# Reciprocal denominators go to the heads' rows through memory in place of a matmul; keys are spread by 8 transfers per group in place of 16

## The chip, the core and the metric

One Trainium2 chip, one of its NeuronCores. The metric is the device time of one execution of the kernel in microseconds (us). The engines are named as the profile names them: PE (TensorE matmul), PEld (TensorE weight load), DVE (VectorE), ACT (ScalarE), POOL (GpSimd), SP (SyncE, here only an issuer of transfers).

## What is computed

8192 tokens (128 sequences of 64) with 128 features: a layernorm, cross attention with 16 heads of width 8 against a context of the same size, a residual; then a layernorm and a feed-forward layer in which each token goes to the one of 8 experts with the largest router logit, and a residual. Cut to what matters here:

```python
q = split_heads(layernorm(x) @ Wq.T + bq)      # 16 heads, width 8
k = split_heads(ctx @ Wk.T + bk)
v = split_heads(ctx @ Wv.T + bv)
scores = einsum('bhqd,bhkd->bhqk', q, k) / sqrt(8)
out = einsum('bhqk,bhkd->bhqd', softmax(scores), v)
x = x + merge_heads(out) @ Wo.T + bo
n = layernorm(x);  e = argmax(n @ Wr.T + br)
x = x + (relu(n @ W1[e].T + b1[e]) @ W2[e].T + b2[e])
```

All data are float32.

## The kernel before

**Stage 1** (about 0 to 68 us) runs over 16 groups of 512 tokens (`GW`; four tiles of 128, `GT`). It normalises x, turns it, and makes Q, K and V for the group with four kinds of matmul (L886, L890, L899, L907); ACT copies them to `QT`, `KT` and `V`.

**Stage 2** (about 68 to 352 us) is a pipeline written out by hand. In step n of 81, tile n of 128 tokens (two sequences) gets its scores (PE, L877), their maximum and the difference to it (DVE, L698 and L706) and the exponential (ACT, L546). In the same step PE turns the exponentials of tile n-2 in two halves of four transposes (L918); ACT copies each half out of the one PSUM bank that both use (L529, L538), so the second half waits for the copy of the first. Then PE makes numerators (L994) and denominators (L1003) of tile n-3.

Denominators of a group of four tiles g are collected in one PSUM bank: row 8h+t holds those of head h, tile t. DVE takes the reciprocal of the whole bank (`RD`, L702, 128x128) once per group, in step 4g+7 (`L_RD`), between its maximum and its subtraction. One step later the first of the group's four tiles needs them: for each tile, PE multiplies a constant selector `C_SEL` by `RD` (L948), which copies row 8h+t to all eight rows of head h, into PSUM bank 7; DVE multiplies that by the numerators `NUM` (L722, `OT`). One step later again PE applies Wo (L952) and DVE adds the residual (L725). Tile m is multiplied in step m+8 (`L_MUL`) and added in step m+9 (`L_X1`). Behind that follow, with eight tiles per batch, the second layernorm's sums, the router's logits (transposes L977, copy L535 to `X1T`, matmul L959), ranks (L966, L968) and the rows' places, and POOL scatters the rows to a DRAM scratch `rows` (L466). DVE works in program order; so do PE, ACT and POOL.

**Keys.** The scores' moving operand `KM` is block diagonal per head: SP copies, for each group s, each head's eight partitions of `KT` to their slot, 16 transfers of 8 partitions x 2 KB (L341), in a loop over s. Group s may be copied once the scores of group s-2 are done. Group 0's 16 copies are issued by POOL (L410). `KM` has room for two groups, and is filled with zeros by POOL in stage 1.

**SP's queue** after stage 1: the copies of keys for s = 1 to 15; then the pad rows and the experts' first weights `WE` (L348), `W2` (L350), seven pads to `rows` (L353), and the blocks of sorted rows, one transfer per block of 128 rows with a register load before each (L362).

**Stage 3** (from step 67, `F0`, about 335 us, to the end) handles 71 blocks of 128 sorted rows. Up to step 80 its blocks are interleaved with what is left of stage 2, one block per step: DVE normalises (L832), PE turns (L1009) and multiplies (L1024, L1037), ACT copies the expert's weights (L559) and applies relu (L563), and POOL scatters the result to `out` (L473).

Of the kernel before, what the change touches and what calls it, by code (L numbers as in the profile page):

```python
# [44 lines left out]
C_ID, C_TRI, C_ONE, C_OWN, C_DEN, C_SEL, C_PREF, C_BASE, C_LIM, C_BLK, C_EPS, C_1H, C_LE, C_END = np.cumsum(  # L45
    [0, P, P, P, 2 * DK, GT * 64, GT * P, E, E, NT, NB, 1, ST, E * E]).tolist()
# [5 lines left out]
def constants():  # L52
# [12 lines left out]
    for t in range(GT):  # L65
        c[:, C_SEL + P * t:C_SEL + P * (t + 1)] = (p[:, None] // DK == p[None, :] // DK) & (p[:, None] % DK == t)
# [100 lines left out]
def build(nc, x, ctxT, wts, we, w2, con, pad, ids, out):  # L167
# [3 lines left out]
    rows = nc.dram_tensor("rows", (ROWS, RW), f32).ap()  # L171

    ctx = ExitStack()
    with ctx:
# [20 lines left out]
        BQK = W[:, W_BQ:W_BQ + 2]  # L195
        WR, BR = W[:, W_R:W_R + E], W[:, W_BR:W_BR + E]

        X1T = sb("X1T", P, 4, 2, P)
# [37 lines left out]
        RD = sb("RD", P, 2, P)  # L236
        OT = sb("OT", P, 2, P)
# [37 lines left out]
        con_in, w_in, ids_in, w2_in = sem("con_in"), sem("w_in"), sem("ids_in"), sem("w2_in")  # L275
# [15 lines left out]
        num_kept, rdx_done, wr_mm, wr_ready = (sem(n) for n in ("num_kept", "rdx_done", "wr_mm", "wr_ready"))  # L291
# [19 lines left out]
        def _(sp):  # L311

            def load_group(s):
                def go(before):
# [17 lines left out]
            def spread(s):  # L332
                sp.wait_ge(q_kept, s.n + 1)
                sp.sem_inc(spread_go, 1)
                need(sp, s_done, GT * (s.n - 1))
                sp.sem_inc(spread_go, 1)
                at = bass.ds(s.n * GW, GW)
                for g in range(2):
                    for j in range(HP):
                        own = slice(SEQ * g + DK * j, SEQ * g + DK * (j + 1))  # L340
                        sp.dma_start(KM[own, s.r, j, :], KT[own, at]).then_inc(km_in[s.r], 16)  # L341
            steps(sp, 1, NG, 2, spread, peel=2)

# [25 lines left out]
            for n in range(NB1 - E):  # L369
                load_block(0)(Step(n // RR, n % RR, RR))  # L370
# [16 lines left out]
        def _(pool):  # L387
# [8 lines left out]
            def stage1(n):  # L396
# [90 lines left out]
        def _(act):  # L487
# [4 lines left out]

            def root(n, dst, src, slots, mv, sd, rstd):
# [4 lines left out]
            def keep(t):  # L498
# [11 lines left out]
                if isinstance(s.n, int) and s.n == 0:  # L510
                    act.wait_ge(w_in, 16)
# [9 lines left out]
            def softmax(s):  # L521
# [8 lines left out]
                for i in range(4):  # L530
                    j = s.batch(M_TR + 2 * i)
                    if j is not None:
                        act.wait_ge(xt2_done, 4 * j + i + 1)
                        need(act, lgp_done, 4 * j - 3 + i)
                        nc.scalar.copy(X1T[:, i].rearrange("p t d -> p (t d)"), bank(6)[:, 2 * P:4 * P]).then_inc(x1t_ready, 1)  # L535
# [45 lines left out]
        def _(dve):  # L581
# [110 lines left out]
            def stage2(s):  # L692
# [17 lines left out]
                need(dve, rdx_done, min(n - L_MUL + 1, NT))  # L710
# [154 lines left out]
        def _(pe):  # L865
# [3 lines left out]
            nc.tensor.matmul(bank(7)[:, D:D + E], C[:, C_ONE:C_ONE + P], WR, start=True, stop=True).then_inc(wr_mm, 1)  # L869

# [12 lines left out]
            def stage1(s):  # L883
                pe.wait_ge(ct_in[s.r], 16 * (s.it + 1))
                need(pe, k_kept, s.n - 1)
                nc.tensor.matmul(bank(4 + s.r % 2), WK, CT[:, s.r, :], start=True, stop=True).then_inc(k_done, 1)  # L886
# [16 lines left out]
                if isinstance(s.n, int) and s.n == NG - 1:  # L903
                    pe.wait_ge(km_first, 16 * H)
                    scores(0)
                need(pe, q_kept, s.n - 1)
                nc.tensor.matmul(bank(2 + s.r % 2), WQ, XNT[:, s.r % 2, :], start=True, stop=True).then_inc(q_done, 1)  # L907
# [13 lines left out]
            def stage2(s):  # L921
                n = s.n
                if 1 <= n < NT:
                    grp, t = divmod(n, GT)
                    if t == 0 and grp:
                        pe.wait_ge(km_in[grp % 2], 16 * H * ((grp + 1) // 2))
# [10 lines left out]
                need(pe, ot_ready, min(n - L_MUL, NT))  # L937
# [159 lines left out]
```

## Time and profile before

| | |
|---|---|
| median of 3 runs | 499.24 us (497.53 to 502.27) |
| the profiled execution | 501.58 us, of which the profile's span is 499.8 us |
| PE busy | 461.1 us (92% of the span) |
| DVE busy | 408.2 us (82%) |
| ACT busy | 313.0 us (63%) |
| POOL busy | 240.6 us (48%) |
| DMA | 33.98 MB, mean 68 GB/s |
| granted TensorE clock | mean 0.98; a slice near 80 us at 0.5 |

Busy times are of one execution on the chip. A busy PE is not PE at its peak: ends of matmuls are modelled, so the timeline of single instructions and what each waited for say more than the share. Times of rows count from the start of the span.

A row of the timeline has start and duration in us, engine, line, operation, output and input, and in brackets how long its engine sat idle before it and what released it. A row of the windows has, for one stretch, its length, the busy us and instructions of PE, PEld, DVE, ACT and POOL in this order, the granted clock, the DMA engines' busy share and GB/s. A row of one line has the duration of an issue (min, median, max in ns), or the us from the start of an issue to its landing. A row of the page's DMA issues ends with the KB of one and the same us. A row of waits has who waited for whom: us in total, times, longest.

### The profile page before, as it was taken

How to read it: one execution, taken by the hardware profiler on the slowest of the kernel's cores; microseconds unless marked ns; L12 is line 12 of the kernel's file. 1: busy time of each engine (PE TensorE's matmuls, PEld its weight loads, DVE VectorE, ACT ScalarE, POOL GpSimd, SP SyncE). 2: the span in 40 equal slices, each digit the busy share in tenths (PEclk: the TensorE clock that was granted, in tenths of full speed). 3: DMA queues.
4: the chain of work that ended last, by engine and by line, in shares of the span. 5: the costliest groups of instructions: out<-in, count | busy, mean ns of one | idle time of the engine just before them, and what ended most of it. 6: DMA issues, size and time to landing. Idle time of an engine off the chain costs nothing. (4 is left out here: it accounts for less than half of the span.)

```text
span 499.8 us, 18728 instructions
## 1 busy us (share of the span) xinstructions
PE 461.1 (92%) x6467; PEld 347.9 (70%) x6467; DVE 408.2 (82%) x1061; ACT 313.0 (63%) x589; POOL 240.6 (48%) x390
## 2 busy tenths in 40 slices
PE   3999978899999999999999999988789999999990
PEld 1666634456666666666666666668779999999990
DVE  4999864677899899998999999958878887887870
ACT  1677764666666666666666665665557777777760
POOL 1548620222232464555645645554767645455551
PEclk9999995999999999999999999999999999999996
DMA  8356300011000111111111115722223332222100
GB/s 281 108 148 177 90 11 12 14 22 20 18 17 18 33 41 30 38 38 36 35 34 33 39 41 201 264 71 76 77 66 103 101 87 66 72 61 74 39 32 0
DMA packets 32752, 33.98 MB, mean 68 GB/s; under 512 B 6675, under 2 KB 26006, under 8 KB 32416
## 3 DMA queue, kind: packets, MB, share of 16 engines
q1 hardware_dynamic: 27840, 24.10, 18.7%
q0 software_dynamic: 4832, 8.80, 5.3%
q8 instruction: 53, 0.87, 0.8%
q14 instruction: 27, 0.22, 0.2%
HBM read 19.14 MB, written 9.99 MB: 58 GB/s over the span
## 5 line engine op out<-in xcount | busy, mean ns | idle before, releaser
L451 POOL TENSOR_TENSOR VP<-BIG,C 128x128 f32<-128x128 f32 x128 | 56.1, 458 | 136.5 <-PE PS L1003 132.7
L918 PEld LDWEIGHTS PS<-C,SB 128*128 128x128 f32 x512 | 54.6, 142 | 68.2 <-ACT SB L546 32.5
L698 DVE TENSOR_REDUCE MX<-PS 128x16 f32<-128x1024 f32 x64 | 78.3, 1223 | 29.1 <-PE PS L877 27.7
L473 POOL DMA_INDIRECT out<-SB,BIG x71 | 70.1, 987 | 52.6 <-DVE SB L849 44.7
L918 PE MATMUL PS<-C,SB 128*128 128x128 f32 x512 | 85.1, 290 | 7.5 <-ACT PT L529 7.2
L546 ACT ACTIVATE SB<-SB 128x1024 f32<-128x1024 f32 x64 | 67.7, 1057 | 23.7 <-DVE SB L706 22.0
L706 DVE TENSOR_TENSOR SB<-PS,MX 128x1024 f32<-128x1024 f32 x64 | 77.4, 1210 | 1.7
L1024 PE MATMUL PS<-BIG,KM 128*128 128x128 f32 x568 | 76.8, 277 | 0.3 <-issue 0.2
L1037 PE MATMUL PS<-KM,SB 128*128 x568 | 75.8, 277 | 0.6 <-ACT SB L563 0.6
L466 POOL DMA_INDIRECT rows<-X,DESTI x64 | 64.2, 1003 | 19.6 <-issue 14.1
L877 PE MATMUL PS<-KM,BIG 64*64 64x512 f32 x512 | 71.2, 629 | 0.8 <-ACT BIG L517 0.8
L559 ACT COPY KM<-BIG 128x644 f32 x71 | 51.7, 729 | 30.2 <-PE PS L1024 24.8
L1024 PEld LDWEIGHTS PS<-BIG,KM 128*128 128x128 f32 x568 | 69.7, 192 | 1.4 <-issue 1.2
L1037 PEld LDWEIGHTS PS<-KM,SB 128*128 128x128 f32 x568 | 69.1, 192 | 1.2 <-issue 0.8
L538 ACT COPY PT<-PS 128x512 f32<-128x512 f32 x64 | 37.5, 586 | 36.7 <-PE PS L918 36.6
L529 ACT COPY PT<-PS 128x512 f32<-128x512 f32 x64 | 37.4, 585 | 36.2 <-PE PS L918 32.8
L838 DVE TENSOR_TENSOR SB<-PS,KM 128x512 f32<-128x512 f32 x71 | 49.0, 690 | 5.4 <-PE PS L1024 2.4
L563 ACT ACTIVATE SB<-SB 128x512 f32<-128x512 f32 x71 | 44.6, 628 | 10.0 <-DVE SB L838 9.7
L994 PE MATMUL PS<-PT,VP 128*32 128x64 f32 x2048 | 42.3, 223 | 0.2
L1003 PE MATMUL PS<-PT,C 128*32 128x128 f32 x1024 | 40.3, 276 | 1.1 <-DVE RD L702 0.7
L994 PEld LDWEIGHTS PS<-PT,VP 128*32 128x32 f32 x2048 | 31.9, 110 | 11.1 <-issue 11.0
L846 DVE TENSOR_TENSOR SB<-PS,KM 128x128 f32<-128x128 f32 x71 | 20.6, 291 | 18.1 <-PE PS L1037 17.2
(122 smaller groups left out, 699.0 us busy)
## 6 DMA issues: line engine op xcount, KB each, us to landing
BIG<-rows SPq DMA_DIRECT2D x71, 66.0 KB, 1.9
X<-in_x SPq DMA_DIRECT2D x16, 256.0 KB, 3.3
PT<-in_ctxT SPq DMA_DIRECT2D x16, 256.0 KB, 3.0
KM<-BIG SPq DMA_DIRECT2D x240, 16.0 KB
BIG<-in_we SPq DMA_DIRECT2D x1, 2576.0 KB, 11.5
KM<-in_w SPq DMA_DIRECT2D x1, 2048.0 KB, 15.9
out<-SB,BIG POOLq DMA_INDIRECT x71, 2.3
rows<-X,DESTI POOLq DMA_INDIRECT x64, 2.4
```

The costliest lines, as they stand in the source:

```text
L451: last = nc.gpsimd.tensor_tensor(dst, v, own, ALU.mult)
L466: nc.gpsimd.indirect_dma_start(out=rows, out_offset=bass.IndirectOffsetOnAxis(ap=DESTI[:, j % 2, t:t + 1], axis=0), in_=X[:, j * ST + t, : ...
L473: nc.gpsimd.indirect_dma_start(out=out, out_offset=bass.IndirectOffsetOnAxis(ap=RT[:, s.r, ID:ID + 1].bitcast(i32), axis=0), in_=YO[:, s.r ...
L546: nc.scalar.activation(SB[:, n % 3, :], SB[:, n % 3, :], ACT.Exp, scale=SCALE).then_inc(exp_done, 1)
L559: nc.scalar.copy(WS[:, s.r % 4, :], WE[:, bass.ds(ex, 1), :].rearrange("p e f -> p (e f)")).then_inc(ws_ready, 1)
L698: nc.vector.tensor_reduce(MX[:, n % 2, :], sc, axis=AX.X, op=ALU.max).then_inc(mx_done, 1)
L706: nc.vector.tensor_tensor(SB[:, n % 3].rearrange("p (h k) -> p h k", h=H), sc, MX[:, n % 2, :].unsqueeze(2).to_broadcast([P, H, SEQ]), ALU ...
L877: last = nc.tensor.matmul(bank(2 * (n % 2) + g)[SEQ * b:SEQ * (b + 1), :], QT[rows_g, n * P + SEQ * b:n * P + SEQ * (b + 1)], KM[rows_g, g ...
L918: last = nc.tensor.transpose(bank(4)[:, i * P:(i + 1) * P], SB[:, n % 3, hp * P:(hp + 1) * P], ident)
L994: nc.tensor.matmul(bank(6)[32 * c:32 * c + 32, at:at + SEQ], VP[:, m % 2, b, 2 * c + z, :], PT[:, m % 2, 2 * c + z, SEQ * b:SEQ * b + SEQ] ...
L1024: last = nc.tensor.matmul(bank(2 + b.r % 2)[:, c * P:(c + 1) * P], WS[:, b.r % 4, c * P:(c + 1) * P], XT[:, b.r % 2, :], start=True, stop= ...
L1037: last = nc.tensor.matmul(bank(4 + b.r % 2)[:, 0:D], HT[:, b.r % 2, c * P:(c + 1) * P], w, start=c == 0, stop=c == FC - 1)
```

## The change

The selector matmul (L948) goes away, and its constant `C_SEL` with it (512 columns, 256 KB of the constants' transfer). In its place SP does, once per group, `ratios(g)`: it waits for the reciprocal, writes `RD` (64 KB) to a DRAM scratch `ratio`, waits for that to land, and reads it back with each of a head's four rows repeated to the head's eight partitions, into `RDX` (128 partitions x 2 KB, 256 KB). DVE waits for that second transfer before it multiplies, and reads `RDX` in place of PSUM. `RDX` has room for two groups. `ratios(s-2)` stands behind the keys' copies of group s; `ratios(14)` stands before the pads, and `ratios(15)` behind the first eight loads of blocks.

The columns of Wq and Wk are put in another order on chip (two copies by ACT at the start, into `RDX`, which is free then), with which one partition of each head lies every 8 partitions. So a transfer `KM[j:P:8]` <- `KT[j:P:8]` takes two heads at once with 16 partitions, and there are 8 per group. The biases come in the same order by two transfers of their own. SP's loop over groups is written out. `WE` and `W2` are issued by ACT in place of SP, in steps 58 and 61. `X1T` has two slots in place of four, and PE waits for `W2` two steps later.

```diff
-C_ID, C_TRI, C_ONE, C_OWN, C_DEN, C_SEL, C_PREF, ...
+C_ID, C_TRI, C_ONE, C_OWN, C_DEN, C_PREF, ...
...
+    ratio = nc.dram_tensor("ratio", (2, P, P), f32).ap()
...
-        BQK = W[:, W_BQ:W_BQ + 2]
+        BQK = sb("BQK", P, 2)
+        def turned(w):
+            return w.rearrange("p (g j d) -> p g d j", g=2, j=HP)
...
-        X1T = sb("X1T", P, 4, 2, P)
+        X1T = sb("X1T", P, 2, 2, P)
...
+        RDX = sb("RDX", P, 2, GT, P)
...
+                        for g in range(2):
+                            own = slice(SEQ * g, SEQ * (g + 1))
+                            sp.dma_start(BQK[own, :], wts[own, W_BQ:W_BQ + 2].rearrange("(j d) b -> d j b", j=HP)).then_inc(b_in, 16)
                         sp.dma_start(IDS[:], ids).then_inc(ids_in, 16)
...
-            def spread(s):
-                sp.wait_ge(q_kept, s.n + 1)
+            def ratios(g):
+                sp.wait_ge(rd_done, g + 1)
+                need(sp, rdx_in[g % 2], 16 * (g // 2))
+                sp.dma_start(ratio[g % 2], RD[:, g % 2, :]).then_inc(rd_out[g % 2], 16)
+                need(sp, ot_ready, GT * (g - 1))
+                sp.wait_ge(rd_out[g % 2], 16 * (g // 2 + 1))
+                of = ratio[g % 2].rearrange("(h a) q -> h a q", a=DK)[:, 0:GT, :].rearrange("h t q -> h (t q)")
+                sp.dma_start(RDX[:, g % 2].rearrange("p t q -> p (t q)"), of.unsqueeze(1).to_broadcast([H, DK, GT * P])).then_inc(rdx_in[g % 2], 16)
+
+            for s in range(1, NG):
+                sp.wait_ge(q_kept, s + 1)
                 sp.sem_inc(spread_go, 1)
-                need(sp, s_done, GT * (s.n - 1))
+                need(sp, s_done, GT * (s - 1))
                 sp.sem_inc(spread_go, 1)
-                at = bass.ds(s.n * GW, GW)
-                for g in range(2):
-                    for j in range(HP):
-                        own = slice(SEQ * g + DK * j, SEQ * g + DK * (j + 1))
-                        sp.dma_start(KM[own, s.r, j, :], KT[own, at]).then_inc(km_in[s.r], 16)
-            steps(sp, 1, NG, 2, spread, peel=2)
+                for j in range(HP):
+                    sp.dma_start(KM[j:P:HP, s % 2, j, :], KT[j:P:HP, s * GW:(s + 1) * GW]).then_inc(km_in[s % 2], 16)
+                if s >= 2:
+                    ratios(s - 2)
...
             sp.dma_start(PADR[:], pad).then_inc(padr_in, 16)
-            sp.dma_start(WE[:], we).then_inc(we_in, 16)
-            sp.wait_ge(s_done, NT - GT)
-            sp.dma_start(W2, w2).then_inc(w2_in, 16)
+            ratios(NG - 2)
             sp.wait_ge(padr_in, 16)
...
             for n in range(NB1 - E):
+                if n == 8:
+                    ratios(NG - 1)
                 load_block(0)(Step(n // RR, n % RR, RR))
...
-                    for k in range(4 * (n - 8), 4 * (n - 7)):
-                        g, j = divmod(k, HP)
-                        own = slice(SEQ * g + DK * j, SEQ * g + DK * (j + 1))
-                        pool.dma_start(KM[own, 0, j, :], KT[own, 0:GW]).then_inc(km_first, 16)
+                    for j in range(2 * (n - 8), 2 * (n - 7)):
+                        pool.dma_start(KM[j:P:HP, 0, j, :], KT[j:P:HP, 0:GW]).then_inc(km_first, 16)
...
+            act.wait_ge(w_in, 16)
+            for k, w in enumerate((WQ, WK)):
+                last = nc.scalar.copy(RDX[:, 0, k, :].rearrange("p (g d j) -> p g d j", g=2, d=DK), turned(w))
+            last.then_inc(w_turned, 1)
...
                 softmax(Step(n // ST, n % ST, ST))
+                if n == NT - 6:
+                    for r in range(2):
+                        act.wait_ge(km_in[r], 16 * HP * (NG // 2 - 1 + r))
+                    act.dma_start(WE[:], we).then_inc(we_in, 16)
+                if n == NT - 3:
+                    act.wait_ge(s_done, NT - GT)
+                    act.dma_start(W2, w2).then_inc(w2_in, 16)
...
                     dve.wait_ge(od_done, GT * g + GT)
+                    need(dve, rdx_in[g % 2], 16 * (g // 2))
                     nc.vector.reciprocal(RD[:, g % 2, :], bank(5)[:, P * (g % 2):P * (g % 2) + P]).then_inc(rd_done, 1)
...
-                need(dve, rdx_done, min(n - L_MUL + 1, NT))
...
                 if 0 <= m < NT:
+                    g, t = divmod(m, GT)
                     dve.wait_ge(num_kept, m + 1)
-                    nc.vector.tensor_tensor(OT[:, m % 2, :], bank(7)[:, 0:P], NUM[:, m % 8, :], ALU.mult).then_inc(ot_ready, 1)
+                    dve.wait_ge(rdx_in[g % 2], 16 * (g // 2 + 1))
+                    nc.vector.tensor_tensor(OT[:, m % 2, :], RDX[:, g % 2, t, :], NUM[:, m % 8, :], ALU.mult).then_inc(ot_ready, 1)
...
+            pe.wait_ge(w_turned, 1)
...
-                m = n - L_MUL
-                if 0 <= m < NT:
-                    g, t = divmod(m, GT)
-                    pe.wait_ge(rd_done, g + 1)
-                    nc.tensor.matmul(bank(7)[:, 0:P], C[:, C_SEL + P * t:C_SEL + P * (t + 1)], RD[:, g % 2, :],
-                                     start=True, stop=True).then_inc(rdx_done, 1)
...
-            pe.wait_ge(w2_in, 16)
             pe.wait_ge(tab_ready, 1)
             for n in range(F0, STEPS):
                 k = n - F0
+                if k == 2:
+                    pe.wait_ge(w2_in, 16)
```

## Rows read from the trace of the kernel before

**Rows 1.** windows of busy time by engine, eight steps of stage 2
```profile
178.80:210.90 32.10, 31.97 (x579) 21.45 (x578) 30.12 (x64) 20.40 (x37) 17.62 (x38) 1.00 0.16 36
```

**Rows 2.** timeline of two steps: PE, PEld and ACT
```profile
200.32 1.09 PE L877 MATMUL PS<-KM,BIG 64*64 64x512 f32 x8
...
201.34 0.66 PE L918 MATMUL PS<-C,SB 128*128 128x128 f32 x4
...
201.84 0.39 PE L948 MATMUL PS<-RD,C 128*128 128x128 f32 x2
...
202.04 0.58 ACT L529 COPY PT<-PS 128x512 f32<-128x512 f32 x1 [0.79 <-PE PS L918]
...
202.67 0.42 PEld L918 LDWEIGHTS PS<-C,SB 128*128 128x128 f32 x4 [0.24 <-ACT PT L529]
...
206.00 0.58 ACT L529 COPY PT<-PS 128x512 f32<-128x512 f32 x1 [0.79 <-issue]
...
206.63 0.42 PEld L918 LDWEIGHTS PS<-C,SB 128*128 128x128 f32 x4
```

**Rows 3.** timeline, ACT and PEld in a step with the ranks' matmuls
```profile
222.13 0.58 ACT L529 COPY PT<-PS 128x512 f32<-128x512 f32 x1 [0.73 <-PE PS L918]
...
222.95 0.42 PEld L918 LDWEIGHTS PS<-C,SB 128*128 128x128 f32 x4
```

**Rows 4.** timeline of DVE around two reciprocals
```profile
194.71 0.95 DVE L702 RECIPROCAL RD<-PS 128x128 f32<-128x128 f32 x1
...
197.52 1.22 DVE L698 TENSOR_REDUCE MX<-PS 128x16 f32<-128x1024 f32 x1 [0.20 <-PE PS L877]
...
199.92 0.28 DVE L722 TENSOR_TENSOR OT<-PS,NUM 128x128 f32<-128x128 f32 x1
...
201.48 1.22 DVE L698 TENSOR_REDUCE MX<-PS 128x16 f32<-128x1024 f32 x1 [0.88 <-PE PS L877]
...
210.92 0.95 DVE L702 RECIPROCAL RD<-PS 128x128 f32<-128x128 f32 x1
...
216.05 0.28 DVE L722 TENSOR_TENSOR OT<-PS,NUM 128x128 f32<-128x128 f32 x1
```

**Rows 5.** the page's DMA issues: the experts' first weights
```profile
BIG<-in_we SPq DMA_DIRECT2D x1, 2576.0 KB, 11.5
```

**Rows 6.** line L325, context loads, 256 KB each
```profile
DMA to landing us min/median/max: 2.6/3.0/6.2
```

**Rows 7.** waits of SP's queue, 374 to 400 us: last pad's write
```profile
SPq L382 <- DMA rows<-BIG: 1.1, 1, 1.1
```

**Rows 8.** line L466, 300 to 325 us: scatters while WE, W2 load
```profile
DMA to landing us min/median/max: 2.3/6.0/7.5
```

**Rows 9.** lines L341, and L362 from 326 to 336 us: SP's issues
```profile
L341 SPq DMA_DIRECT2D KM<-BIG x240: 645/646/1555, 54.5 to 301.9; - x120
...
L362 SPq DMA_DIRECT2D BIG<-rows x8: 350/352/365, 326.8 to 335.0; - x8
```

**Rows 10.** timeline, 304 to 341 us: SP, ACT, DVE around last reciprocals
```profile
304.40 1.57 SPq L348 DMA_DIRECT2D BIG<-in_we  x1
...
305.28 1.06 ACT L546 ACTIVATE SB<-SB 128x1024 f32<-128x1024 f32 x1 [0.92 <-DVE SB L706]
...
307.71 0.95 DVE L702 RECIPROCAL RD<-PS 128x128 f32<-128x128 f32 x1
...
313.55 0.28 DVE L722 TENSOR_TENSOR OT<-PS,NUM 128x128 f32<-128x128 f32 x1
...
325.18 0.95 DVE L702 RECIPROCAL RD<-PS 128x128 f32<-128x128 f32 x1
...
329.27 0.29 DVE L722 TENSOR_TENSOR OT<-PS,NUM 128x128 f32<-128x128 f32 x1 [1.47 <-PE PS L959]
...
337.00 0.95 DVE L702 RECIPROCAL RD<-PS 128x128 f32<-128x128 f32 x1
...
340.07 0.29 DVE L722 TENSOR_TENSOR OT<-PS,NUM 128x128 f32<-128x128 f32 x1 [0.68 <-PE PS L968]
```

More of the change, by code:

```diff
@@ L42 @@
 SCALE = float(1.0 / np.sqrt(np.float32(DK)))
-C_ID, C_TRI, C_ONE, C_OWN, C_DEN, C_SEL, C_PREF, C_BASE, C_LIM, C_BLK, C_EPS, C_1H, C_LE, C_END = np.cumsum(
-    [0, P, P, P, 2 * DK, GT * 64, GT * P, E, E, NT, NB, 1, ST, E * E]).tolist()
+C_ID, C_TRI, C_ONE, C_OWN, C_DEN, C_PREF, C_BASE, C_LIM, C_BLK, C_EPS, C_1H, C_LE, C_END = np.cumsum(
+    [0, P, P, P, 2 * DK, GT * 64, E, E, NT, NB, 1, ST, E * E]).tolist()
 (W_Q, W_K, W_V, W_BQ, W_BK, W_O, W_BV, W_BO, W_R, W_BR, W_END) = np.cumsum(
@@ L64, in constants @@
                 c[half, C_DEN + 64 * t + 32 * z + 16 * z + DK * r + t:C_DEN + 64 * t + 32 * z + 16 * z + DK * (r + 1):GT] = 1
-    for t in range(GT):
-        c[:, C_SEL + P * t:C_SEL + P * (t + 1)] = (p[:, None] // DK == p[None, :] // DK) & (p[:, None] % DK == t)
     c[:, C_PREF:C_PREF + E] = E - np.arange(E)
@@ L272, in bank @@
             return PS[:, 512 * k:512 * (k + n)]
-        con_in, w_in, ids_in, w2_in = sem("con_in"), sem("w_in"), sem("ids_in"), sem("w2_in")
+        con_in, w_in, w_turned, b_in, ids_in, w2_in = sem("con_in"), sem("w_in"), sem("w_turned"), sem("b_in"), sem("ids_in"), sem("w2_in")
         x_in, ct_in = sems("x_in", 4), sems("ct_in", 4)
@@ L290, in build @@
         stat2, mv2, inv_step, scaled = (sem(n) for n in ("stat2", "mv2", "inv_step", "scaled"))
-        num_kept, rdx_done, wr_mm, wr_ready = (sem(n) for n in ("num_kept", "rdx_done", "wr_mm", "wr_ready"))
+        num_kept, wr_mm, wr_ready = (sem(n) for n in ("num_kept", "wr_mm", "wr_ready"))
+        rd_out, rdx_in = sems("rd_out", 2), sems("rdx_in", 2)
         seed_step, sd2_done, inv2_done = sem("seed_step"), sem("sd2_done"), sem("inv2_done")
@@ L330, in _ @@
             sp.wait_ge(zeroed, 8)
-            def spread(s):
-                sp.wait_ge(q_kept, s.n + 1)
+            def ratios(g):
[8 more added lines that the diff above has]
+                sp.wait_ge(q_kept, s + 1)
                 sp.sem_inc(spread_go, 1)
-                need(sp, s_done, GT * (s.n - 1))
+                need(sp, s_done, GT * (s - 1))
                 sp.sem_inc(spread_go, 1)
-                at = bass.ds(s.n * GW, GW)
-                for g in range(2):
-                    for j in range(HP):
-                        own = slice(SEQ * g + DK * j, SEQ * g + DK * (j + 1))
-                        sp.dma_start(KM[own, s.r, j, :], KT[own, at]).then_inc(km_in[s.r], 16)
-            steps(sp, 1, NG, 2, spread, peel=2)
+                for j in range(HP):
+                    sp.dma_start(KM[j:P:HP, s % 2, j, :], KT[j:P:HP, s * GW:(s + 1) * GW]).then_inc(km_in[s % 2], 16)
+                if s >= 2:
+                    ratios(s - 2)
             for r in range(2):
-                sp.wait_ge(km_in[r], 16 * H * (NG // 2 - 1 + r))
+                sp.wait_ge(km_in[r], 16 * HP * (NG // 2 - 1 + r))
             sp.dma_start(PADR[:], pad).then_inc(padr_in, 16)
-            sp.dma_start(WE[:], we).then_inc(we_in, 16)
-            sp.wait_ge(s_done, NT - GT)
-            sp.dma_start(W2, w2).then_inc(w2_in, 16)
+            ratios(NG - 2)
             sp.wait_ge(padr_in, 16)
@@ L510, in keep @@
                 if isinstance(s.n, int) and s.n == 0:
-                    act.wait_ge(w_in, 16)
+                    act.wait_ge(b_in, 16 * 2)
                 act.wait_ge(k_done, s.n + 1)
@@ L533, in softmax @@
                         act.wait_ge(xt2_done, 4 * j + i + 1)
-                        need(act, lgp_done, 4 * j - 3 + i)
-                        nc.scalar.copy(X1T[:, i].rearrange("p t d -> p (t d)"), bank(6)[:, 2 * P:4 * P]).then_inc(x1t_ready, 1)
+                        need(act, lgp_done, 4 * j - 1 + i)
+                        nc.scalar.copy(X1T[:, i % 2].rearrange("p t d -> p (t d)"), bank(6)[:, 2 * P:4 * P]).then_inc(x1t_ready, 1)
                 if 2 <= n < NT + 2:
@@ L885, in stage1 @@
                 need(pe, k_kept, s.n - 1)
-                nc.tensor.matmul(bank(4 + s.r % 2), WK, CT[:, s.r, :], start=True, stop=True).then_inc(k_done, 1)
+                nc.tensor.matmul(bank(4 + s.r % 2), RDX[:, 0, 1, :], CT[:, s.r, :], start=True, stop=True).then_inc(k_done, 1)
                 pe.wait_ge(xn_done, s.n + 1)
@@ L903, in stage1 @@
                 if isinstance(s.n, int) and s.n == NG - 1:
-                    pe.wait_ge(km_first, 16 * H)
+                    pe.wait_ge(km_first, 16 * HP)
                     scores(0)
                 need(pe, q_kept, s.n - 1)
-                nc.tensor.matmul(bank(2 + s.r % 2), WQ, XNT[:, s.r % 2, :], start=True, stop=True).then_inc(q_done, 1)
+                nc.tensor.matmul(bank(2 + s.r % 2), RDX[:, 0, 0, :], XNT[:, s.r % 2, :], start=True, stop=True).then_inc(q_done, 1)
             steps(pe, 0, NG, 4, stage1, peel=4, tail=4)
@@ L925, in stage2 @@
                     if t == 0 and grp:
-                        pe.wait_ge(km_in[grp % 2], 16 * H * ((grp + 1) // 2))
+                        pe.wait_ge(km_in[grp % 2], 16 * HP * ((grp + 1) // 2))
                     need(pe, sub_done, n - 1)
@@ L936, in stage2 @@
                 need(pe, x1_done, min(n - L_X1, NT))
-                need(pe, ot_ready, min(n - L_MUL, NT))
+                if 0 <= n - L_X1 < NT:
+                    pe.wait_ge(ot_ready, n - L_X1 + 1)
                 j = s.routing(M_TOP)
@@ L958, in stage2 @@
                             at = 2 * P + (ST * (j % 2) + 2 * i + t) * E
-                            last = nc.tensor.matmul(bank(7)[:, at:at + E], X1T[:, i, t, :], WR, start=True, stop=True)
+                            last = nc.tensor.matmul(bank(7)[:, at:at + E], X1T[:, i % 2, t, :], WR, start=True, stop=True)
                         last.then_inc(lgp_done, 1)
```

## The prediction

> **What bounds the kernel now.** I read the windows first. In the middle of stage 2, eight steps take 32.1 us, 4.0 us a step, and PE is busy for 31.97 of them at full clock while DVE is busy for 30.12 [rows 1]. Both are near their limit, so a busy share doesn't say what an edit is worth; the timeline does. The reader is to see in [rows 2] that the matmul to be removed stands in a hole. PE ends the first half of the transposes at 201.34 + 0.66 = 202.00. ACT copies it from 202.04 to 202.62, and only then, at 202.67, can the second half begin, after 0.24 us of idle that ends with that copy. From half to half 1.33 us pass, and the selector matmul, Wo and the transposes of X lie inside. In the next step, where two logit matmuls lie in the hole, the copy ends at 206.58 and the second half starts at 206.63: copy and PE's work end together. Only where the ranks' matmuls are added does PE outlast the copy: the copy ends at 222.71, the second half starts at 222.95 [rows 3]. That is one step in eight.
>
> Then DVE. The reciprocal ends at 195.66 and the first product of its group starts at 199.92, 4.26 us later; the next pair is 211.87 and 216.05, 4.18 us [rows 4]. DVE's idle in eight steps is the 0.20 before 197.52 and the 0.88 before 201.48, 1.08 us in all (the other steps show none). These gaps are what two transfers in a row have to fit into.
>
> **The change, part by part.** The sum is made on the profiled execution, 501.6 us; it lies 2.3 us above the median of the runs, 499.2.
>
> *The selector matmul, 64 times.* Its two passes are busy for 0.39 us [rows 2], and it starts 0.16 us before the transposes end, so part of that overlaps with its neighbours; I take half, 0.2 us, as what it adds to PE's work. With it gone, seven steps of eight wait for ACT's copy exactly as before: 0. In the rank step it gives back at most 222.95 - 222.71 = 0.24, of which 0.05 is the copy's handover [rows 3]: 0.19 us, for about seven batches 1.3 us. DVE's product reads the core's memory in place of PSUM; no row shows this to be shorter, and I take 0.28 us for both [rows 4].
>
> *The two transfers, in the middle.* The write of 64 KB: the last pad, 66 KB from SP to DRAM, was waited for 1.1 us after its issue [rows 7], and an issue takes 0.35 [rows 9]: 1.45 us. From above, a scatter of 66 KB, POOL's own work in it, takes 2.3 us in quiet [rows 8]. The read of 256 KB in pieces of 2 KB: the context's loads have size and pieces, 2.6 to 3.0 us [rows 6]. Handovers DVE to SP, SP to SP and back: 0.04 to 0.05 each in [rows 2]; I take 0.3 for the three. So 4.35 us from below (1.45 + 2.6 + 0.3) and 5.6 from above (2.3 + 3.0 + 0.3); I take 4.8, near the rows of the same issuer. What may it be? In eight steps DVE meets the wait twice, and with its idle gone the gaps are 4.26 - 0.20 and 4.18, 8.24 us. PE's eight steps are 32.1 - 0.19, and DVE without idle needs 32.1 - 1.08, so 0.89 us of delay is free: 2 x trip = 9.13, a trip of 4.57 is hidden. With 4.8 the loss is 0.46 us in eight steps, with 5.6 it is 2.1, with 4.35 nothing and the 0.19 remain. For seven times eight steps: 3 us, between -1.3 and 14. I take 4, since other transfers use the same engines in some of the trips. SP has nothing else to do then; what is queued behind its wait is the next group's keys. What waits behind DVE's wait is Wo of the step after and the next maximum.
>
> The Trainium skill (DMA: Bandwidth & Descriptors, Anatomy of one DMA) puts a transfer at about 2.0 us and its bytes by 436 GB/s. An estimate by it is 2.15 + 2.6 + 0.3 = 5.05 us, and a loss of 7 us in place of 4; the section also says that completion is slowest where the target is the chip's DRAM, which would put the write above the pad's 1.45 us.
>
> *The keys.* An issue takes 0.645 us on SP [rows 9]. Sixteen were at least 10.3 us per group, eight are 5.2, or 10.3 if twice the rows cost twice. Group g+3 may start when the scores of step 4g+7 are done, but now SP first serves the reciprocal of that step: up to 1.7 us to its start (the maximum takes 1.2 [rows 4]), 0.95, 1.6 for the write, 0.4 to issue the read, 4.7 us in all. With the issues and up to 3 us to land that is 13 us (18 at twice the cost); five steps less one set of scores, 5 x 4.0 - 1.1 = 19 us, are there. Hidden: 0. Without that cover PE would stand at the group's first scores.
>
> *The start.* The constants shrink by 256 KB; at the rate of the 2576 KB that landed in 11.5 us [rows 5] that is 1.1 us of transfer, if the start is bound by it. Two small transfers and two weight copies on ACT come in. I take -0.5, between -1 and +1.
>
> *WE moved to ACT, with reciprocal 13.* ACT issues it behind the exponential of step 58, which ends at 306.34 [rows 10]. The issue took SP 1.57 us and now holds ACT's copies of step 59 for that long. More dearly, the load then meets the write of reciprocal 13 (ends at 308.66). In the kernel before, scatters of the same size that met these loads took 6.0 us in the middle and up to 7.5, against 2.3 [rows 8]. So the write takes about 6.5, lands at 315.3, and the read 3 to 4 more: the trip is some 10 to 11 us. The product that waits stands at 313.55, 4.9 us after the reciprocal: 5.5 us late. ACT's 1.57 lies beside that, and about 0.5 is absorbed: +5. From below +1 (the transfers don't hinder each other), from above +8.
>
> *Reciprocal 14.* It ends at 326.13; its product starts at 329.27 after an idle of 1.47 [rows 10]. A trip of 5 to 7 us (W2, issued by ACT in step 61, is then still loading) ends 2 to 4 us after that, and DVE's idle in that step and what a step without scores leaves free take most: +1.5, between 0 and 3.
>
> *Reciprocal 15.* Here SP itself is late. Pads and loads now stand behind ratios(14). The write lands and the read is issued 2 us after 326.13; seven pads at the 0.35 to 0.6 of an issue, 4 us: the first block's load goes out at about 332, which the first block just bears (it is wanted in step 67, the step of reciprocal 15). Eight loads come at (335.0 - 326.8) / 7 = 1.17 us [rows 9], to 341.5. But the reciprocal ends at 337.95 and its product stood at 340.07 [rows 10]. Write at 341.5, landed with the read at 346: 6 us late, 3 if SP were free. DVE's blocks stand behind the product, and PE and ACT wait for them; nothing there covers 6 us. +5.5, between 2.5 and 7.
>
> *The last steps of stage 2.* After the last scores a step is a loop between PE and DVE through bank 7 (the product at 329.27 was released by PE). A matmul less is 0.2 us in about eight steps: -1.5, at least 0.
>
> Sum, with the rank steps' 1.3 us inside the 4: -0.5 + 4 + 5 + 1.5 + 5.5 - 1.5 = +14 us, 515.6 on the profiled execution and 513.2 on the median; the prediction is for the median, rounded up to 514.
>
> **Rivals.**
>
> *PE gives the matmul back (faster).* If the copy did not end the hole, every step would be 0.2 us shorter: 64 x 0.2 = 13 us, 487. For it: PE is busy for 31.97 of 32.1 us [rows 1]. Against it: the 0.24 us of idle on the copy [rows 2], half of all steps; and DVE has only 1.08 us in eight steps to follow. It decides if the trip stays below 4.57 us and PE's hole isn't bound by the copy. 0.1, some gain in other places included.
>
> *Hidden (within 1%).* The trips are 4.3 us, and in the tail the loads hinder them little: -1.3 - 0.5 + 1 + 0 + 2.5 - 1.5 = 0: 499 to 503. For it: the pad's 1.45 us and the 2.6 us at the low end [rows 6, 7]. 0.2.
>
> *Much slower.* The trip is 5.6 in the middle (14 us), and the loads hold reciprocal 13 to the end of WE: 14 - 0.5 + 8 + 3 + 7 = 31 us, 530. The Trainium skill (DMA: Bandwidth & Descriptors, Queues, rings and completion order) has each DMA engine change between queues only after a whole packet of some 9 to 17 descriptors, by which the write would stand behind all of WE's rows. By rows, WE lands 11.5 us after its issue [rows 5] near 306.4, so at about 318, and the read ends at 321: 7.5 us late in place of 5.5. 0.15, with it a loss of PE's clock in the new idle.
>
> **Numbers.** The forecast has 0.55, and 503 to 526 as its own range; faster 0.1, hidden 0.2, much slower 0.15. The range is to leave out no more than 0.2: faster and a part of the much slower, 498 to 527. About 1%, 5 us, is what can be told from no change: faster 0.12, within 0.18, slower 0.7.
>
> **What would show it.** In the profile after: DVE's product of each group's first tile idle before it, released by a DMA into `RDX`, 0.3 to 1 us, and the idle before the next maximum gone; eight steps of 32.5 us; PE with idle between the halves of the transposes; SP's keys never waited for by L877; one wait of 5 us at step 60 while WE loads and one of 5 to 6 at step 68. If the waits on `RDX` are absent in the middle, the trip was overestimated; if eight steps take under 31.5 us, the hole was read wrongly; if step 60 shows no long wait, the two queues don't hinder each other.

## The result, and the profile after

| | before | changed |
|---|---|---|
| median | 499.21 us (497.53 to 502.52, 6 runs) | 518.67 us (517.06 to 526.37, 6 runs) |
| ratio | | 1.0399, 95% interval 1.0354 to 1.0444 |
| profiled execution, span | 501.58, 499.8 us | 518.43, 516.6 us |

The change makes the kernel 4.0% slower, 19.5 us in the medians. Forecast were 514 us, 498 to 527. All ratios compare fast executions with fast ones of the kernel before, measured beside them, so they differ a little from the quotient of the medians; the 526.37 us is a slow one.

First the middle, the same eight steps as in all that follows (from the maximum of tile 24 to that of tile 32); columns as in [rows 1].

```profile
162.80:196.00 33.20, 31.23 (x562) 20.13 (x563) 30.32 (x64) 20.17 (x37) 17.79 (x38) 1.00 0.18 55
```

33.2 us where [rows 1] has 32.1. PE has 0.74 us less of work in them and takes 1.1 us longer. Not every eight steps are alike: from the maximum of tile 40 to that of tile 48 they take 32.2 us and the next eight 33.9. Over the 48 steps from 8 to 56 it is 33.0 us for eight, and 32.1 in the kernel before. The hole between the transposes' halves is as in [rows 2]: first half to 212.97, copy to 213.58, second half from 213.63, in the changed kernel's timeline:

```profile
212.31 0.66 PE L946 MATMUL PS<-C,SB 128*128 128x128 f32 x4
...
213.00 0.58 ACT L547 COPY PT<-PS 128x512 f32<-128x512 f32 x1
...
213.63 0.42 PEld L946 LDWEIGHTS PS<-C,SB 128*128 128x128 f32 x4 [0.20 <-ACT PT L547]
```

The new wait, in the same view: the reciprocal of step 47, then the first product of its group, then the next maximum, which no longer waits (compare [rows 4]).

```profile
258.79 0.95 DVE L728 RECIPROCAL RD<-PS 128x128 f32<-128x128 f32 x1
...
265.82 0.29 DVE L749 TENSOR_TENSOR OT<-RDX,NUM 128x128 f32<-128x128 f32 x1 [1.82 <-DMA RDX<-ratio]
...
266.43 1.21 DVE L723 TENSOR_REDUCE MX<-PS 128x16 f32<-128x1024 f32 x1
```

From the reciprocal's end to the product are 6.08 us here; over the twelve trips of the middle it is 4.9 to 6.2, 5.5 in the mean, and DVE waits 1.25 us of each. The list of waits has the sum: all 16 groups are waited for.

```profile
DVE OT L749 <- DMA RDX<-ratio: 30.2, 16, 5.7
```

Then the end of stage 2. WE's issue, reciprocal 13, SP's two issues and the product in step 60:

```profile
307.67 0.40 ACTq L589 DMA_DIRECT2D BIG<-in_we  x1
...
310.23 0.95 DVE L728 RECIPROCAL RD<-PS 128x128 f32<-128x128 f32 x1
311.20 0.33 SPq L343 DMA_DIRECT2D ratio<-RD  x1
...
318.02 0.55 SPq L347 DMA_DIRECT2D RDX<-ratio  x1
...
321.60 0.29 DVE L749 TENSOR_TENSOR OT<-RDX,NUM 128x128 f32<-128x128 f32 x1 [5.26 <-DMA RDX<-ratio]
```

SP's next issue comes 6.8 us after that of the write, and PE stands idle for 5.5 us before Wo (L975), which needs the product (timeline of PE):

```profile
322.97 0.77 PE L975 MATMUL PS<-W,OT 128*128 128x128 f32 x2 [5.53 <-DVE PREF L680]
```

Reciprocal 15 in step 67 and its product in step 68:

```profile
348.14 0.95 DVE L728 RECIPROCAL RD<-PS 128x128 f32<-128x128 f32 x1
...
351.21 0.37 SPq L343 DMA_DIRECT2D ratio<-RD  x1
352.93 0.55 SPq L347 DMA_DIRECT2D RDX<-ratio  x1
356.23 0.29 DVE L749 TENSOR_TENSOR OT<-RDX,NUM 128x128 f32<-128x128 f32 x1 [5.71 <-DMA RDX<-ratio]
```

SP issues the write 2.1 us after the reciprocal's end (349.09), since it is still at the eight loads.

Where the time went in the two profiled executions, by how much later the same instruction starts than before (maxima and products of DVE, DVE's first instruction of the last block):

| stretch | later by | of it here |
|---|---|---|
| to the first maximum | +0.1 | +0.1 |
| steps 0 to 4 | -3.9 | -4.0 |
| steps 4 to 59 | +2.5 | +6.4 |
| step 60 (reciprocal 13) | +8.05 | +5.5 |
| steps 61 to 63 | +9.1 | +1.1 |
| steps 64 and 65 (reciprocal 14) | +10.1 | +1.0 |
| steps 66 and 67 | +11.1 | +1.0 |
| step 68 (reciprocal 15) | +16.2 | +5.0 |
| to the last block | +17.1 | +0.9 |

The second line is not the change's doing as far as can be told; without it the lines add up to 21 us. From 75 to 87 us the kernel before ran at a mean clock of 0.57 in its profiled execution (first row) and the changed one at full clock (second row), with the same instructions behind the transposes of 76 us:

```profile
75.00:87.00 12.00, 9.59 (x81) 4.69 (x82) 5.48 (x5) 5.53 (x9) 0.86 (x2) 0.57 0.06 12
```

```profile
75.00:87.00 12.00, 8.83 (x144) 4.79 (x144) 7.98 (x7) 8.00 (x13) 1.74 (x4) 1.00 0.08 23
```

The same window has 0.72 in the profiles of e5 and e10 and 1.00 in that of e2, so kernels with and without the transfers show either. The kernel before comes in both kinds by its mean clock: of its 19 executions measured beside e1, those with a mean clock of 0.991 or 0.992 took 497.6 to 499.2 us, those with 0.981 or 0.982 took 501.4 to 502.7, and the profiled one (501.58 us, 0.982) is of the second kind. On the other side the changed kernel has two stretches at the lower level (1.2 GHz) that the kernel before has not, one around PE's idle in step 60 and one around the wait in step 68 (e1 and e2 below, which have no such wait, show one too, between 333 and 348 us):

```profile
320.00:327.00 7.00, 4.03 (x60) 3.32 (x64) 5.12 (x16) 1.93 (x4) 0.00 (x0) 0.51 0.13 37
347.00:361.00 14.00, 8.16 (x43) 7.52 (x44) 6.74 (x29) 4.16 (x9) 1.27 (x3) 0.52 0.30 78
```

### The profile page after: what moved, and what is told of

It reads as the page before. It is cut to its first block and busy times, and to the rows that moved or that the text cites. A ratio compares the mean times of both kernels' runs of the same rounds, so it can differ in the third digit from the quotient of the medians.

```text
span 516.6 us, 18138 instructions
## 1 busy us (share of the span) xinstructions
PE 454.2 (88%) x6339; PEld 338.9 (66%) x6339; DVE 408.7 (79%) x1061; ACT 312.4 (60%) x591; POOL 237.4 (46%) x382
## 5 line engine op out<-in xcount | busy, mean ns | idle before, releaser
L464 POOL TENSOR_TENSOR VP<-BIG,C 128x128 f32<-128x128 f32 x128 | 57.6, 469 | 143.1 <-PE PS L1026 139.2
L946 PE MATMUL PS<-C,SB 128*128 128x128 f32 x512 | 83.9, 287 | 13.7 <-ACT PT L547 11.1
L1047 PE MATMUL PS<-BIG,KM 128*128 128x128 f32 x568 | 78.8, 281 | 0.3 <-issue 0.2
L479 POOL DMA_INDIRECT rows<-X,DESTI x64 | 64.4, 1006 | 19.5 <-issue 13.1
L1047 PEld LDWEIGHTS PS<-BIG,KM 128*128 128x128 f32 x568 | 71.6, 196 | 1.4 <-issue 1.2
L905 PE MATMUL PS<-KM,BIG 64*64 64x512 f32 x512 | 69.5, 615 | 0.8 <-ACT BIG L535 0.8
L749 DVE TENSOR_TENSOR OT<-RDX,NUM 128x128 f32<-128x128 f32 x64 | 24.0, 375 | 32.1 <-DMA RDX<-ratio 30.2
L975 PE MATMUL PS<-W,OT 128*128 128x128 f32 x128 | 27.9, 301 | 16.7 <-DVE PREF L680 8.6
```

The source lines that it names most:

```text
L464: last = nc.gpsimd.tensor_tensor(dst, v, own, ALU.mult)
L479: nc.gpsimd.indirect_dma_start(out=rows, out_offset=bass.IndirectOffsetOnAxis(ap=DESTI[:, j % 2, t:t + 1], axis=0), in_=X[:, j * ST + t, : ...
L905: last = nc.tensor.matmul(bank(2 * (n % 2) + g)[SEQ * b:SEQ * (b + 1), :], QT[rows_g, n * P + SEQ * b:n * P + SEQ * (b + 1)], KM[rows_g, g ...
L946: last = nc.tensor.transpose(bank(4)[:, i * P:(i + 1) * P], SB[:, n % 3, hp * P:(hp + 1) * P], ident)
L1047: last = nc.tensor.matmul(bank(2 + b.r % 2)[:, c * P:(c + 1) * P], WS[:, b.r % 4, c * P:(c + 1) * P], XT[:, b.r % 2, :], start=True, stop= ...
```

## The experiments

**Is the matmul worth anything?** e1: the kernel before, the matmul out, nothing in its place.

```diff
-                    nc.tensor.matmul(bank(7)[:, 0:P], C[:, C_SEL + P * t:...], RD[:, g % 2, :], ...)
...
-                    nc.vector.tensor_tensor(OT[:, m % 2, :], bank(7)[:, 0:P], NUM[:, m % 8, :], ALU.mult)
+                    nc.vector.tensor_tensor(OT[:, m % 2, :], C[:, C_SEL:C_SEL + P], NUM[:, m % 8, :], ALU.mult)
```

> The kernel before with the selector matmul taken out and nothing in its place: DVE multiplies the numerators by a constant, so the attention's rows are not divided by their denominators (the part left out). Theory (the matmul stood in the hole of ACT's copy): only the rank steps and the last steps get shorter, -1.3 and -1.5 us, so 496 to 499 us, and eight steps of the middle take 31.9 to 32.1 us. Rival (PE sets every step): 64 x 0.2 = 13 us less, about 486 us, and eight steps of 30.5 us.

Measured 501.2 us beside 500.5 for the kernel before, ratio 1.0016 (0.9976 to 1.0056). Windows of the eight steps:

```profile
162.85:194.81 31.96, 30.62 (x562) 19.82 (x562) 30.30 (x64) 20.16 (x37) 17.89 (x38) 1.00 0.15 36
```

PE's busy time falls from 31.97 us [rows 1] to 30.62, 1.35 us, and the stretch only from 32.14 us (the same eight steps, 165.38 to 197.52 before) to 31.96. The rival is gone: a PE busy for 99.6% of the time had 1.35 us of its work in a hole. The rank step's 0.19 us is there. The 1.5 us of the last steps are not seen: from step 59 to 66 the kernel without the matmul gains under 0.1 us on the kernel before, and behind that it has a stretch at the lower level (336 to 345 us) which the kernel before has not.

**Is it the transfers?** e2: the changed kernel with the matmul back; the transposed weights in a tile of their own.

```diff
-                if s >= 2:
-                    ratios(s - 2)
...
-                    nc.vector.tensor_tensor(OT[:, m % 2, :], RDX[:, g % 2, t, :], NUM[:, m % 8, :], ALU.mult)
+                    nc.vector.tensor_tensor(OT[:, m % 2, :], bank(7)[:, 0:P], NUM[:, m % 8, :], ALU.mult)
...
+                    nc.tensor.matmul(bank(7)[:, 0:P], C[:, C_SEL + P * t:...], RD[:, g % 2, :], ...)
```

> The changed kernel with the selector matmul back in place of the two transfers; keys by 8 transfers, turned weights and the weights' loads on ACT stay. Theory (the transfers through memory cost it all): eight steps of 32.1 us, no wait of 5 us in steps 60 and 68, 498 to 502 us in all. Rival (keys' transfers, the turned weights or ACT's issues cost a part): 503 us or more.

498.0 us, ratio 0.9966 (0.9934 to 0.9999), eight steps of 32.1 us. The transfers cost all of it; keys by 8 transfers and the weights' loads on ACT cost nothing that can be seen. Its lead of a third of a percent is at the edge of the interval, too small to be called a gain.

**Is it the trip's length?** e3 leaves out one leg, e4 adds one.

```diff
-                sp.dma_start(ratio[g % 2], RD[:, g % 2, :]).then_inc(rd_out[g % 2], 16)
-                sp.wait_ge(rd_out[g % 2], 16 * (g // 2 + 1))
-                of = ratio[g % 2].rearrange(...)
+                of = ctxT[0:H, 0:GT * P]
```

> The changed kernel without the write to memory and the wait for it: the read follows the reciprocal at once and takes another tensor of the same shape and pieces, so the denominators do not reach the rows (the part left out). The trip becomes about 3.5 us in place of 5.3. Theory (length of the trip against a gap of 4.6 us): no wait on RDX in the middle, eight steps of 31.9 us, 5 to 6 us less there; in step 60 and 68 the waits go down by the write's time, 5 and 2 us; about 505 us in all. Rival (contention of the transfers with others, or the new wait's order costs it, whatever its length): 515 us or more.

```diff
                 sp.dma_start(ratio[g % 2], RD[:, g % 2, :]).then_inc(rd_out[g % 2], 16)
+                sp.wait_ge(rd_out[g % 2], 16 * (2 * (g // 2) + 1))
+                sp.dma_start(ratio[g % 2], RD[:, g % 2, :]).then_inc(rd_out[g % 2], 16)
...
-                sp.wait_ge(rd_out[g % 2], 16 * (g // 2 + 1))
+                sp.wait_ge(rd_out[g % 2], 16 * (2 * (g // 2) + 2))
```

> The changed kernel with the write done twice, one after the other has landed: 1.9 us more per trip. Theory (DVE pays every us beyond what its idle covers, twice in eight steps): eight steps are 3.8 us longer than in the changed kernel, 36 to 37 us; 16 x 1.9 = 30 us more in all, about 548 us, some 5 more where the weights load. Rival (the wait is mostly absorbed by other slack): under 530 us.

e3: 505.9 us, 1.0101 (1.0037 to 1.0164), 31.98 us in eight steps and no wait on `RDX` before step 60. e4: 554.4 us, 1.1053 (1.0983 to 1.1122); its trips are 6.5 to 8.7 us, and eight steps take 38.3 us, or 36.8 in a stretch at full clock. First e3, then two windows of e4:

```profile
162.20:194.18 31.98, 30.63 (x562) 19.83 (x562) 30.32 (x64) 20.18 (x37) 17.90 (x38) 1.00 0.17 53
```

```profile
174.30:212.60 38.30, 32.31 (x562) 21.31 (x563) 29.96 (x65) 20.48 (x37) 18.14 (x38) 0.96 0.17 51
290.40:327.20 36.80, 31.32 (x563) 20.16 (x563) 29.95 (x66) 20.21 (x37) 18.03 (x38) 1.00 0.17 52
```

One leg, two legs, three legs: 31.9, 33.0 and 37.4 us for eight steps in the mean of steps 8 to 56. The first leg is free. The second is paid in part: DVE waits 1.25 us for each trip, and eight steps, with two trips, are 0.9 us longer than before. The third is paid in full: the trips are 2.1 us longer in the mean, and eight steps 4.4 us, of which a lower clock in places has a part. In e3 the read of 256 KB per group still runs, and in e9 below both transfers do, at 32.0 us: it is the wait that costs, not the traffic.

**Is it WE in step 60?** e5 moves the issues of WE and W2 later, e11 puts them back on SP, where they stand behind reciprocal 13.

```diff
-                if n == NT - 6:
+                if n == NT - 4:
...
                     act.dma_start(WE[:], we).then_inc(we_in, 16)
-                if n == NT - 3:
+                if n == NT:
```

> The changed kernel with the issue of WE two steps later (step 60) and that of W2 three steps later (step 64), so that the write of reciprocal 13 has gone before WE starts and WE has landed before that of reciprocal 14. Theory (the 5.3 us wait in step 60 is the write queued beside WE): the trip of reciprocal 13 goes from 10.4 us to about 5.5, the wait in step 60 to under 1 us; W2 now loads beside nothing or beside reciprocal 14's read; 513 to 515 us in all. Rival (something else in step 60 is late, ACT's issue above all): the wait stays, 518 us.

```diff
             sp.dma_start(PADR[:], pad).then_inc(padr_in, 16)
+            sp.dma_start(WE[:], we).then_inc(we_in, 16)
+            sp.wait_ge(s_done, NT - GT)
+            sp.dma_start(W2, w2).then_inc(w2_in, 16)
             ratios(NG - 2)
...
-                    act.dma_start(WE[:], we).then_inc(we_in, 16)
...
-                    act.dma_start(W2, w2).then_inc(w2_in, 16)
```

> The changed kernel with the issues of WE and W2 back on SP, behind the pad's load and ahead of ratios(14), so behind reciprocal 13's transfers; all else as changed. Theory (the 5.3 us wait in step 60 is the meeting of the write with WE, and the loads are done before the blocks' loads start): the trip of reciprocal 13 goes from 10.4 to 5.5 us and nothing takes its place in step 67, where e5 waited 5.9 us; 513 to 514 us in all. Rival (the loads then hinder reciprocal 14 by as much): 517 us or more.

e5: 519.3 us, 1.036 (1.0287 to 1.0433). The cause is confirmed and the gain is not. The trip of reciprocal 13 goes from 10.4 to 5.5 us and the wait to 0.32; but then the first block's rows are waited for. Their load is issued at 343.3 us, while W2 (issued at 337.87, 10.6 us to landing) is still in flight (timeline of DVE in e5):

```profile
321.45 0.38 DVE L749 TENSOR_TENSOR OT<-RDX,NUM 128x128 f32<-128x128 f32 x1 [0.32 <-DMA RDX<-ratio]
...
350.96 0.35 DVE L859 TENSOR_SCALAR BIG<-BIG 128x128 f32<-128x128 f32 x1 [5.92 <-DMA BIG<-rows]
```

By these times the collision moved from step 60 to step 67, where I had not looked. e11: 516.6 us, 1.033 (1.0296 to 1.0363): no wait in step 60 (trip 5.1 us), 1.25 us for the first block, and reciprocal 14 as in the changed kernel. Of the 5.3 us some 2 come back in the median, 3.5 by the ratios, whose intervals overlap.

**Is it SP's order in step 68?** e6 serves reciprocal 15 behind six loads.

```diff
-                if n == 8:
+                if n == 6:
                     ratios(NG - 1)
```

> The changed kernel with reciprocal 15 served behind six loads of blocks in place of eight. Theory (of the 7.1 us of that trip 2.1 are SP's lateness): the trip goes to about 5.1 us, the wait in step 68 from 5.7 to 3.7, 516 to 517 us in all. Rival (SP's order does not matter there, or the later loads of blocks 6 and 7 are then waited for): 518.5 us or more.

519.7 us, 1.0398 (1.0326 to 1.047), and not the expected 516 to 517. The trip goes from 7.1 to 5.2 us and the wait from 5.7 to 3.8, as expected; the time shows nothing that its interval can tell. In the profile the product of step 68 is 14.0 us later than before where it was 16.2, but two steps on it is 16.0 where it was 17.0, so half of the gain is gone by then. SP's lateness was 2 of the 5.7 us, the rest is the trip itself.

**Are the keys late?** e8 spreads them by 16 transfers again.

```diff
-                for j in range(HP):
-                    sp.dma_start(KM[j:P:HP, s % 2, j, :], KT[j:P:HP, ...])
+                for g in range(2):
+                    for j in range(HP):
+                        at = slice(SEQ * g + j, SEQ * (g + 1), HP)
+                        sp.dma_start(KM[at, s % 2, j, :], KT[at, ...])
```

> The changed kernel with the keys spread by 16 transfers of 8 partitions per group as before, everything else as changed. Theory (SP has time for both): PE never waits for keys, the middle's eight steps stay at 33 us, 518 to 520 us; at the end ACT's wait for the last keys ahead of WE may be met, up to 1.5 us. Rival (halving the transfers was what made room for the new ones): keys late for each group, 2 to 3 us per group, 550 us.

520.7 us, 1.0399 (1.0347 to 1.0451), not to be told from the changed kernel. PE never waits for keys in either. The eight steps from tile 24 took 34.2 us and not 33, but from step 4 to 59 it is 228.0 us beside 227.2, so little of that is the keys'. The halving was not needed for SP to serve the new transfers.

**Can the trip be covered?** e7 puts product and residual one step later, e9 the routing too, e10 serves reciprocal 15 behind four loads, e12 adds e11's order.

```diff
-L_MUL = 8
-L_X1 = 9
+L_MUL = 9
+L_X1 = 10
...
-SOON = 2
+SOON = 1
```

(`SOON` is by how many steps the routing of the last two batches runs ahead of the others' place.)

> The changed kernel with product and residual one step later (steps m+9 and m+10, and the last batches' routing one step later with them), so that the trip has a gap of about 8.5 us. Theory (trip against gap): no wait on RDX in the middle, eight steps of 31.97 us, 5 to 6 us less there; in step 60 (now 61) the wait goes from 5.3 to about 2 us, in step 68 (now 69) from 5.7 to about 3; the additional step at the end costs 2 to 3 us; 507 to 511 us in all. Rival (the transfers hurt also where DVE does not wait for them): 514 us or more.

512.9 us, 1.026 (1.0211 to 1.0309). No product of the middle waits any more, and still the eight steps take 33.1 us. My expectation of 32.0 failed. The timeline of DVE in e7 shows another cause: moments (L612 to L620) and seed (L772 to L778) now fall into one step, and the maximum after them, the reciprocal and the subtraction start late; the idle stands in other steps.

```profile
205.19 0.36 DVE L612 TENSOR_TENSOR MS<-STAT 128x8 f32<-128x8 f32 x1
...
207.35 0.17 DVE L778 TENSOR_SCALAR HALF<-VAR 128x8 f32<-128x8 f32 x1
207.55 1.22 DVE L723 TENSOR_REDUCE MX<-PS 128x16 f32<-128x1024 f32 x1
208.69 0.95 DVE L728 RECIPROCAL RD<-PS 128x128 f32<-128x128 f32 x1
...
212.76 1.22 DVE L723 TENSOR_REDUCE MX<-PS 128x16 f32<-128x1024 f32 x1 [1.44 <-PE PS L905]
```

e9 tells that from the transfers: product and residual as in e7, SOON back to 2, all of the routing's offsets one more, so that only the last batches keep e7's places.

```diff
-M_SEED = 18
-M_INV = (19, 20)
+M_SEED = 19
+M_INV = (20, 21)
...
-M_TOP = 21
-M_HOT = 22
-M_RANK = 22
-M_POS = 23
-M_OUT = 23
+M_TOP = 22
+M_HOT = 23
+M_RANK = 23
+M_POS = 24
+M_OUT = 24
```

> The changed kernel with product and residual one step later as in e7_step_later, and also all of the routing's work (square root's seed, top, ranks, places) one step later, so that the moments and the seed are again in different steps. Theory (in e7 eight steps took 33.1 us without any wait on RDX because moments and seed, 2.3 us of DVE, fell into one step right before the reciprocal's 0.95): eight steps go back to about 32.0 us, 507 to 509 us in all. Rival (the transfers themselves slow the other engines down): eight steps stay at 33 us, 512 to 513 us.

505.9 us, 1.012 (1.0093 to 1.0146), and the eight steps:

```profile
162.10:194.10 32.00, 30.73 (x563) 19.89 (x562) 30.44 (x65) 20.21 (x37) 17.52 (x37) 1.00 0.18 55
```

The same DVE work (30.44 us against 30.52 in e7) placed otherwise is worth 1.1 us in eight steps, and 7 us in all. From step 4 to 59 e9 takes 219.8 us, e7 227.9 and the kernel before 220.8: with the trips covered the middle is 1.1 us shorter than before, near the 1.3 us that the rank steps were to give.

e10 is e9 with one more edit:

```diff
-                if n == 8:
+                if n == 4:
                     ratios(NG - 1)
```

> As e9_routing_later, with reciprocal 15 served behind four loads of blocks in place of eight. In e7 SP issued its write 4.3 us after the reciprocal and DVE waited 5.5 us. Theory: the wait goes to about 1 us, 503 to 505 us in all. Rival (the loads that now come later are waited for instead): 507 us or more.

501.6 us, 1.0022 (1.0000 to 1.0044). The wait for reciprocal 15 goes from 5.11 us in e9 to 1.36, and 4 us go from the time. This is the changed kernel with its trips covered but for two short waits, and it is no faster than the kernel before.

e12 is e10 with the issues of WE and W2 on SP as in e11.

> As e10_routing_later_r15, with the issues of WE and W2 on SP behind reciprocal 13 as in e11_weights_on_sp. Theory: the last wait on RDX outside the last group's, 0.9 us in step 61, goes away, and nothing else moves: 500 to 501 us in all, not to be told from the kernel before (the routing's additional step costs what the rank steps give back). Rival (with every wait covered, the removed matmul now shows): under 495 us.

500.8 us, 1.0049 (1.0016 to 1.0083), beside 498.1 for the kernel before. The 0.9 us in step 61 went, but reciprocal 14 is then waited for 3.3 us and the first block 1.9. No gain over e10.

## Why the prediction was right, step by step

The sum said +14 us, measured are +19.5 in the medians and +16.9 in the profiled executions, +21 there without the early stretch at the lower clock. The way, its two places in the end and their order of size were right; several terms were off. Of the 7 us that the sum is short of the 21, 3.6 are the last steps' and 2.4 the middle's.

- *Selector matmul, in a hole: 0, and 0.19 us in the rank step.* Right. e1 has 31.96 us for 32.14.
- *Two transfers in the middle: +4.* Measured +6.4 between steps 4 and 59. The trip was mis-sized: 4.8 taken, 5.5 us measured. The write took 1.8 us in the median (1.5 to 2.9) for 1.45, the read 3.2 (3.1 to 3.5) for about 2.8. The rule by which a longer trip is paid charges nearly twice too much: by 2 x (5.5 - 4.57), less the rank step's 0.19, eight steps should have lengthened by 1.7 us, measured are 0.9 in the mean of steps 8 to 56. So two errors partly cancel, and that this term came near is in part luck. Why the rule charges too much no run shows. The Trainium skill's 2.0 us and bytes by 436 GB/s (DMA: Bandwidth & Descriptors, Anatomy of one DMA) are given there for transfers that GpSimd issues, and these are SP's. The estimate by it was 2.15 for the write, above its 1.5 in quiet, and 2.6 for the read, below its 3.2; for the sum of both it was nearer than I.
- *Keys: 0.* Right, by e8.
- *Start: -0.5.* It is +0.1. The constants land in 3.8 us in place of 4.2, and nothing waits less for it.
- *WE beside reciprocal 13: +5.* Right in size (+5.5 in step 60) and in cause (e5, e11: the trip falls from 10.4 to 5.5 and 5.1 us). How the load holds the write is another matter: I took 6.5 us for the write from scatters that met the loads, and what the runs show is the rival's way, the write held to the end of WE. The two came out alike by luck: the write was issued 3.5 us after WE where the rows had the reciprocal's end 2.3 after it, and WE was out of the way 10.35 us after its issue in place of 11.5. ACT's issue was not 1.57 us but 0.40; that term was nil. What I missed is that removing the collision does not give its 5 us back.
- *Reciprocal 14: +1.5.* +1.0.
- *Reciprocal 15: +5.5.* +5.0, of which SP's order 2 in that step (e6), the trip the rest. With two steps of cover and SP on time 4 us came back (e9 to e10).
- *The last steps: -1.5.* Not seen: steps 61 to 63 and 66 to 67 are longer by 1.1 and 1.0 us, partly at the lower clock, and in e1 nothing is gained either. That is the term whose sign was wrong, and the largest miss of the sum; what lengthens these steps no run shows.
- *The clock* stood among the risks of the slow rival only. In the two profiled executions it gives 4 us to the changed kernel at the start and takes an unknown part in steps 61 to 68. What it does to the medians stays open: the early stretch comes and goes between kernels with the same instructions, and no experiment holds it fixed. It is large enough to hide a small difference: the fastest executions of e10 and e12 are 499.5 and 499.0 us, those of the kernel before beside them 497.5 and 497.6.

## What to carry to other kernels

A busy share of 99.6% did not make the matmul worth removing: look for what ends the idle just after the work you mean to remove, and whether that stays where it is. A round trip through memory is to be set against the time between producer and first consumer on the waiting engine; here 5.5 us against 4.3, and only moving the consumer a step later, without piling up other work of that engine, made it free. When a collision is cleared by moving one party, ask whom the moved one meets next.

## What the runs showed of the hardware

**A small transfer issued while a large one was in flight on another queue ended when the large one did.** WE (2.6 MB, ACT's queue) took 10.2 us in e9 (issued at 300.20) and 9.4 in e7 (issued at 305.63). The 64 KB write that SP issued 3.6 and 5.0 us later was followed by SP's next issue 10.4 and 9.7 us after WE's issue. The issues of SP, first in e9, then in e7:

```profile
303.84 0.33 SPq L343 DMA_DIRECT2D ratio<-RD  x1
310.58 0.55 SPq L347 DMA_DIRECT2D RDX<-ratio  x1
```

```profile
310.60 0.33 SPq L343 DMA_DIRECT2D ratio<-RD  x1
315.31 0.55 SPq L347 DMA_DIRECT2D RDX<-ratio  x1
```

The later it is issued, the shorter it takes, 6.7 and 4.7 us. In the changed kernel, e4, e6, e8 and e10 SP's next issue came 10.2 to 10.5 us after WE's as well. In e3 the small one is the read of 256 KB, issued 3.4 us after WE: 7.4 us to landing, where the reads of the changed kernel take 3.1 to 3.5. By the Trainium skill (DMA: Bandwidth & Descriptors, Queues, rings and completion order) a DMA engine changes queues only between packets, typically of about 9 to 17 descriptors. That would hold the write behind all of WE's rows if an engine's share of them were one packet. These runs agree in that the write is held to WE's end; its packets they do not show.

**Writes that met a load of instructions took longer.** DMA of the changed kernel from 127.92 to 130.8 us, then from 161 to 162.6: the write of 64 KB took 2.9 us where a load of instructions ran beside it and 1.5 without.

```profile
q8 instruction: 1, 0.02, 2.8%
issues: line engine op xcount, KB each, median us to landing
ratio<-RD SPq DMA_DIRECT2D x1, 64.0 KB, 2.9
```

```profile
q1 hardware_dynamic: 144, 0.07, 13.9%
issues: line engine op xcount, KB each, median us to landing
ratio<-RD SPq DMA_DIRECT2D x1, 64.0 KB, 1.5
```

From SP's issue of the write to its next issue, the 13 writes of the middle take 1.5 to 1.6 us where no such load ran beside them (five) and 1.9 to 2.9 us where one did (seven); one more, with a load only at its end, took 1.6. No experiment removed the loads, so that they are the cause is not shown. It is the slow writes by which the term of 1.45 us fell short.
